# Causal attention stage: the query, key and value projections as three products of rounded parts

## The reference, cut to what matters

```python
q = jnp.einsum('btm,mhd->bhtd', x, wq)
k = jnp.einsum('btm,mhd->bhtd', x, wk)
v = jnp.einsum('btm,mhd->bhtd', x, wv)
q = frac_rope(q) * D_HEAD ** (-0.5)
k = frac_rope(k) * D_HEAD ** (-0.5)
s = jnp.einsum('bhid,bhjd->bhij', q, k)
s = s - NEG * jnp.less(i, j).astype(s.dtype)
p = jax.nn.softmax(s, axis=-1)
o = jnp.einsum('bhij,bhjd->bhid', p, v)
return jnp.einsum('bhid,hdm->bim', o, wo)
```

## Time and profile before

| what | before |
|---|---|
| median of three runs | 1653.03 us |
| the three runs | 1645.95, 1653.03, 1653.17 us |
| the profiled execution, its own time | 1644.63 us |
| its span in the profile | 1642.8 us |
| TensorE busy in the span | 1518.9 us (92%) |
| VectorE, ScalarE, GpSimd busy | 1130.2, 802.5, 580.0 us |
| mean granted TensorE clock | 0.977 of full |

### The profile page before, as it was taken

How to read it: one execution, slowest core, us unless ns; L and a number is a source line. 1 busy time by engine, 2 the same in 40 slices (tenths; PEclk the granted TensorE clock), 3 DMA queues, 4 the chain that set the end, 5 groups by cost and what they waited for, 6 DMA issues and landing times.

```text
span 1642.8 us, 34390 instructions
## 1 busy us (share of the span) xinstructions
PE 1518.9 (92%) x12742; PEld 1354.4 (82%) x12742; DVE 1130.2 (69%) x2350; ACT 802.5 (49%) x1527; POOL 580.0 (35%) x684
## 2 busy tenths in 40 slices
PE   4888888899999999888889799999989999989997
PEld 2777777799999999777777588888879999989997
DVE  3899987756655655227888558877867767766674
ACT  5777742244544454235676544545434444443442
POOL 3666650212111210047777212111104444443443
PEclk9999999899999999989999899999999999999999
DMA  5222253212333321062323141222134463554443
GB/s 190 65 78 77 70 192 122 78 44 86 97 97 102 102 97 33 27 211 70 98 79 112 52 160 56 66 66 62 44 74 99 100 132 83 117 113 86 108 91 66
DMA packets 118159, 152.11 MB, mean 93 GB/s; under 512 B 10090, under 2 KB 102852, under 8 KB 117508
## 3 DMA queue, kind: packets, MB, share of 16 engines
q1 hardware_dynamic: 110068, 127.48, 28.1%
q0 software_dynamic: 6560, 19.02, 4.0%
q10 hardware_dynamic: 1392, 3.70, 0.6%
HBM read 111.37 MB, written 38.80 MB: 91 GB/s over the span
## 4 chain that ended last, share of the span: by engine, by line
PE 47%; ACT 5%; issue 2%; DVE 2%; DMA 1%; POOL 0%; SPq 0%; ACTq 0%; POOLq 0%; DVEq 0%
PE psum L531 21%; PE psum L1861 4%; PE psum L1449 4%; PE psum L1845 3%; PE psum L498 3%; PE psum L506 3%; PE psum L1839 2%; PE psum L1822 2%; ACT arena_y L1549 1%; PE psum L490 1%; PE psum L2209 1%; ACT arena_y L1566 1%; PE psum L1496 1%; PE psum L1481 1%; ACT arena_y L1403 1%
## 5 line engine op out<-in xcount | busy, mean ns | idle before, releaser
L2189 POOL TENSOR_TENSOR d_g_parts<-arena_w,d_g_parts 128x512 fp32r<-128x512 f32 x128 | 165.3, 1291 | 249.1 <-ACT d_g_parts L2321 249.1
L531 PE MATMUL psum<-d_v_high,d_g_parts 128*128 128x256 f32 x1024 | 203.9, 283 | 3.0 <-DVE arena_x L1979 2.9
L531 PE MATMUL psum<-d_x_parts,d_v_high 128*128 128x256 f32 x1024 | 193.8, 287 | 7.6 <-issue 6.1
L531 PE MATMUL psum<-m_w_high,m_h_parts 128*128 128x256 f32 x1024 | 188.0, 284 | 0.0
L1213 ACT ACTIVATE arena_x<-psum,b_e 128x512 f32<-128x512 f32 x128 | 88.3, 690 | 189.6 <-PE psum L531 89.6
L531 PEld LDWEIGHTS psum<-d_x_parts,d_v_high 128*128 128x128 f32 x1024 | 159.2, 191 | 14.6 <-issue 8.4
L1141 POOL DMA_INDIRECT arena_x<-x_d,slot_row x64 | 67.1, 1049 | 293.3 <-PE psum L1187 229.1
L531 PEld LDWEIGHTS psum<-d_v_high,d_g_parts 128*128 128x128 f32 x1024 | 167.5, 190 | 3.7 <-issue 3.0
L2329 ACT ACTIVATE arena_y<-psum 128x512 f32<-128x512 f32 x128 | 76.4, 597 | 182.8 <-PE psum L531 182.7
L531 PE MATMUL psum<-m_xF_parts,m_w_high 128*128 128x512 f32 x512 | 159.8, 394 | 2.1 <-DVE m_xF_parts L526 2.1
L531 PEld LDWEIGHTS psum<-m_w_high,m_h_parts 128*128 128x128 f32 x1024 | 160.7, 192 | 0.0
(11 more groups left out here) (281 smaller groups left out, 3644.0 us busy)
## 6 DMA issues: line engine op xcount, KB each, us to landing
arena_x<-wT_d SPq DMA_DIRECT2D x128, 256.0 KB, 5.4
arena_y<-in_L_ffn_w SPq DMA_DIRECT2D x16, 1024.0 KB, 8.0
x_d<-arena_x SPq DMA_DIRECT2D x32, 256.0 KB, 2.2
y_d<-arena_x SPq DMA_DIRECT2D x16, 512.0 KB, 9.0
arena_x<-kv_d SPq DMA_DIRECT2D x16, 512.0 KB, 3.3
kv_d<-arena_x SPq DMA_DIRECT2D x9, 512.0 KB, 2.9
arena_x<-in_x SPq DMA_DIRECT2D x16, 256.0 KB, 2.9
arena_x<-in_ctx SPq DMA_DIRECT2D x16, 256.0 KB, 3.0
```

Of the source, the lines that this page charges most:

```text
L531: ins = nc.tensor.matmul(dst, left[a_], right[b_], start=start and k == 0, stop=stop and k == 2, skip_group_check=True)
L2189: nc.gpsimd.tensor_tensor(K["gP"][:, s % 4, 1], K["g"][:, s % 2], K["gP"][:, s % 4, 0].bitcast(F32), ALU.subtract).then_inc(d_gl, 1)
```

## The change

The input of the projections is kept as two parts, `C["x3P"]`, in place of `C["x3F"]`: the high part is written by ScalarE where it wrote x3F, the low part by a new VectorE instruction that reads bank 0 and the high part. The three weights are split once, ahead of the first step, by three copies and three subtractions on VectorE, into `C["w"]` in an arena that is free there. Each of the 12 f32 matmuls of a unit's projections becomes three matmuls of rounded parts. TensorE waits for the low part (`c_x3l`) where it waited for x3F. In VectorE's list the new instruction stands behind the statistics of u4 and ahead of the moments of u4.

```diff
-        C["x3F"] = arena_y.take([P, NC_, T])
+        C["x3P"] = arena_y.take([P, 2, NC_, T], "c_x3_parts")
...
+        c_x3l, c_wh, c_wl = sem("c_x3l"), sem("c_wh"), sem("c_wl")
...
                 for h in range(H1):
                     for c in range(NC_):
-                        ins = nc.tensor.matmul(bank(k)[:, h * T:(h + 1) * T], w[name][:, c, h * P:(h + 1) * P],
-                                               C["x3F"][:, c, :], start=(c == 0), stop=(c == NC_ - 1))
+                        ins = matmul_split(bank(k)[:, h * T:(h + 1) * T],
+                                           [C["w"][:, name, part, c, h * P:(h + 1) * P] for part in range(2)],
+                                           [C["x3P"][:, part, c, :] for part in range(2)], c == 0, c == NC_ - 1)
...
                 if u1:
                     done(pe, c_x3, u1)
-                    done(pe, c_x3F, u1.back(1))
+                    done(pe, c_x3l, u1.back(1))
                     to_feature(bank(0), C["x3"][:, u1.c % 4]).then_inc(c_x3T, 1)
...
                 if u1:
-                    done(pe, c_x3F, u1)
-                    project(u1, 1, "L1_attn_wq", c_q, (c_qt, c_q2))
+                    if t.fixed and t.n == 2:
+                        pe.wait_ge(c_wl, 3)
+                    done(pe, c_x3l, u1)
+                    project(u1, 1, 0, c_q, (c_qt, c_q2))
...
                         for c in range(NC_):
-                            ins = nc.tensor.matmul(bank(3)[:, b * D:(b + 1) * D], C["x3F"][:, c, b * S:(b + 1) * S],
-                                                   w["L1_attn_wv"][:, c, :], start=(c == 0), stop=(c == NC_ - 1))
+                            ins = matmul_split(bank(3)[:, b * D:(b + 1) * D],
+                                               [C["x3P"][:, part, c, b * S:(b + 1) * S] for part in range(2)],
+                                               [C["w"][:, 2, part, c, :] for part in range(2)], b == c == 0,
+                                               c == NC_ - 1)
...
-                    nc.scalar.activation(C["x3F"], chunks(bank(0)), ACT.Copy).then_inc(c_x3F, 1)
+                    nc.scalar.activation(C["x3P"][:, 0], chunks(bank(0)), ACT.Copy).then_inc(c_x3F, 1)
...
+            for k, name in enumerate(("L1_attn_wq", "L1_attn_wk", "L1_attn_wv")):
+                nc.vector.tensor_copy(C["w"][:, k, 0], w[name][:, :, :]).then_inc(c_wh, 1)
+            for k, name in enumerate(("L1_attn_wq", "L1_attn_wk", "L1_attn_wv")):
+                dve.wait_ge(c_wh, k + 1)
+                low_part(C["w"][:, k, 1], w[name][:, :, :], C["w"][:, k, 0]).then_inc(c_wl, 1)
...
                     ln_bn(dve, u4, C["r4"], C_st4, ln4)
+                if u1:
+                    done(dve, c_x3F, u1)
+                    done(dve, c_v, u1.back(1))
+                    low_part(C["x3P"][:, 1], chunks(bank(0)), C["x3P"][:, 0]).then_inc(c_x3l, 1)
+                if u4:
                     ln_moments(dve, u4, C_st4, ln4)
                     ln_shift(dve, u4, C_st4, ln4)
...
+        C["w"] = arena_x.view("c_w_parts", ARENA_X - 3 * 2 * NC_ * D, [P, 3, 2, NC_, D])
...
-                    for part in (c_x3F, c_qr, c_kr, c_q2, c_k2, c_vs, c_r4):
+                    for part in (c_x3l, c_qr, c_kr, c_q2, c_k2, c_vs, c_r4):
```

More of the change, by code:

```diff
@@ L1488, in step @@
                 if u1:
-                    project(u1, 2, "L1_attn_wk", c_k, (c_kt, c_k2))
+                    project(u1, 2, 1, c_k, (c_kt, c_k2))
                 if u3:
```

## The result

The changed kernel takes 1677.65 us (median of four runs, 1674.94 to 1681.41), the kernel before 1649.49 (four runs, 1644.2 to 1653.17). The ratio is 1.0187 with a 95% interval of 1.0158 to 1.0216: slower by about 28 us. The profiled execution took 1681.41, its span is 1679.6, its mean granted clock 0.960.

A forecast was written before the change was run, and what follows sets the result against it. A chain of waits through TensorE and ScalarE bounded the attention stage; the edit would close a longer loop over VectorE. Loop terms +18.4 and clock falls +5.5 made +24 on the mean 1650.7: 1675 us, range 1657 to 1696.

The forecast's parts named there:

- The loop over VectorE: Attention stage: x3F, low part, VectorE's series, exponentials, next x3F close a loop of 13.11 us, 15.5 over 12 periods.
- a sign of being wrong: Attention stage: prediction wrong if exponentials still start right behind ScalarE's copy of the attention output, or query groups 12.0 or less apart.
- TensorE's saving: Projections: 0.29 us gained each; the 0.58 for queries and keys falls into TensorE's slack of 1.13.
- The clock: TensorE at queries: falls to half clock from thin work before them; 6 falls at 0.9, +5.5 us, bounds 0 and 27.6.
- a period with a fall has less idle time behind it, so I expect falls in half of the periods: Attention stage: the step that set the clock term at 6 falls of 0.9 us.
- the Trainium skill's rule: TensorE before queries: short gaps leave the clock up, clock term zero; rival without falls 1669, chance 0.17.
- GpSimd, next in line: Attention stage: GpSimd's root for u0 complete by 9.3, ScalarE's layernorm result at 9.71 after x3F, 0.4 us away.
- The first periods: Three periods between first query group and 764.74: +3.0 us, bounds 0 and 3.9.
- in the two others the expert sum is pushed back likewise: Second and third of the first three periods: delayed like later ones, while VectorE works slack away in the first.
- the old loop: Attention stage before the edit: TensorE's queries to probabilities by values, then ScalarE to x3F, 11.82 us a period.
- The weights: Splitting ahead of the first step: 3.5 us of VectorE once, covered by its idle time, cost zero.
- the end: Behind the last query group: 0.74 added, 3 x 0.29 taken away, -0.1 us.

The follow-up runs named there:

- experiment 5: The kernel before, f32 products kept, plus only the new VectorE instruction, writing a difference nothing reads, which TensorE waits for: 1670.66 us, ratio 1.0140.
- 4: The changed kernel without VectorE's low-part instruction; TensorE waits for ScalarE's copy and the split products read the high part instead: 1650.86 us, ratio 1.0026.
- experiment 1: The changed kernel with maximum and bias of the scores moved ahead of the rotation of q in VectorE's list: 1670.98 us, ratio 1.0166.
- 3: The changed kernel with six extra matmuls, result unread, behind each output projection to fill TensorE's idle time: 1667.66 us, ratio 1.0123.
- experiment 2: The changed kernel with the low part moved behind moments and shift of u4 in VectorE's list: 1671.78 us, ratio 1.0152.
- experiment 6: The kernel before, with ScalarE's copy of v moved behind its copy x3F of the next unit: 1636.02 us, ratio 0.9939.
- experiment 10: The changed kernel with u4 moments before low part, bias before q rotation, v copy behind next x3 copy, plus three filling matmuls at queries: 1652.55 us, ratio 1.0027.

## Why the prediction was right, and where it was not

**The loop over VectorE.** Predicted 13.11 a period, found 13.02 and 13.03 where the clock stayed up, and 12.9 to 13.14 in experiment 5. Counted from the periods at full clock, the order in VectorE's list accounts for 12 x 1.205 = 14.5 us of the 24.0; the term was 15.5. Shown by 5 (the loss without the split products), by 4 (no such loss without the instruction) and by the last period of 1. But the prediction had named a sign of being wrong, exponentials right behind ScalarE's copy of the attention output, and ten of the twelve periods show it (854.97 and 855.46 above), with queries and keys in the chain: there TensorE's path, made longer by the fall, is the later one. The 14.5 is therefore what VectorE's order costs at full clock, and not what would come back if it alone were undone; experiment 1 undid it and got 0.1 a period.

**TensorE's saving falls into slack.** 1.43 to 1.44 a projection, as forecast; with a fall TensorE is late enough to count, by half a microsecond or more; without one it has a microsecond to spare. Filling matmuls in 3 cost nothing.

**The clock.** Right in kind, too small. I had taken six falls of 0.9, 5.5 in all, and found ten of twelve periods with one. Against 13.03 the eight short falls cost about 0.47 each, near the 0.5 that I had worked out, and the two long ones 1.5 and 1.8 (I had 2.3): 7.1 together. The late starts of ScalarE, 0.20, 0.47 and 1.71, are no falls; they make the other 2.4 of the remaining 24.0 - 14.5 = 9.5, and the prediction had no term for them. The step that failed is "a period with a fall has less idle time behind it, so I expect falls in half of the periods". The first half of it is true: from output projection to queries it is 3.65 to 4.08 us behind a period with a fall, and 4.7 behind one at full clock. But seven of the eight periods with a short fall were followed by another fall. That the Trainium skill's rule (TensorE: Matmul & The Clock Gate, section Why this matters for your kernels), by which short idle gaps keep the clock up, would make the term zero is not borne out here: no idle piece above 1.20 us lay between output projection and queries in the stretch up to 861.8, and queries ran at half clock behind it. What lay there were two groups of turns and no other product for 3.7 us, against 2.6 us in the kernel before, which had no fall in twelve periods. The length of that stretch alone doesn't decide it either: two others, 4.1 and 3.65 us long and made up alike, had full clock behind them (stretch, length, busy, clock, DMA).

```profile
872.90:877.00 4.10, 1.35 (x9) 1.00 0.00 0
901.20:904.80 3.60, 1.31 (x8) 1.00 0.00 0
```

Which of these stretches is followed by a fall is open. The falls come with TensorE's longer wait and not with the shorter products: with the wait and f32 products (5) eight of twelve periods have one, with split products and without the wait (4) two.

**GpSimd, next in line.** Predicted 0.4 us away. It did not show in the changed kernel, and became the bound at 12.7 when VectorE was moved away; the prediction's own terms give 0.74 + 0.57 + 0.16 + 6.82 + 1.02 + 3.38 = 12.7.

**The first periods.** I had +3.0 for the three periods up to the fourth x3F; they took 34.2 instead of 34.3. The first lasts 8.57 against 8.55, the second 12.25 against 11.79, the third 13.37 against 13.97. The step "in the two others the expert sum is pushed back likewise" failed: these periods were not on the old loop to begin with, one of them was 13.97 long by a fall of the clock, and TensorE's shorter products helped there. This error and what the clock and the late starts cost beyond the forecast nearly cancel.

**The weights.** Zero, as forecast. The stage's first instructions are 1.2 us late, and so is the experts' stage before it, ahead of every edit.

**The total.** 1675 against 1677.65. The stage was forecast at +24 and gives +23.2: the loop 14.5 (forecast 15.5), falls 7.1 (5.5), late starts 2.4 (nothing), the first periods -0.1 (+3.0), the end -0.7 (-0.1). The longer last stage was not forecast at all. The kernel became slower for the reason given; that the total is off by less than 3 us is in part luck, since parts that were off by 1 to 3 us each make each other up.

## What to carry to other kernels

A wait put into an in-order engine's list delays everything behind it in that list; follow the list down to the next instruction that the loop needs, and add the time to the loop, whatever the added instruction itself costs. Here 0.7 us of work became 1.2 us a period because a series of 6 us was tied to an event that it did not depend on before. When one engine of a loop has slack, making it faster gives nothing. And where TensorE is the one made to wait, the clock can fall besides.

## What I had not expected of the hardware

- Falls of TensorE's clock to half in ten periods of twelve, though no idle piece ahead of the queries was longer than 1.2 us in eight of them and 1.7 us in the two others; and a kernel with more matmuls being faster by 10 us.
- ScalarE, standing idle, started up to 1.95 us behind the end of the product it waited for, in some periods of the kernels with split products. In the kernel before and in experiment 2 it did not; with f32 products it was 0.38 once in experiment 5 and 0.21 once in experiment 6. Its cause is open; in experiment 10, of what the three moves could give (11.5 a period), it keeps back about one us a period.
- The last stage's wait for its transfers differs by up to 42 us between kernels that are identical there (10.4 to 52.3 in the profiles), while the stage's length moves by 10 at most. It is the least in the kernels with f32 projections and the most in those with filling matmuls.
